# Two decoder stacks in a software pipeline: turning the queries before the scores, with the vector and GpSimd order around them rearranged

## The reference

```python
qkv = x @ Wqkv                       # 128 -> 3 * 1024, 16 heads of 64
q = l2norm(q) * qs;  k = l2norm(k) * ksc
q = q * cos * scale + rotate_half(q) * sin * scale
k = k * cos / scale + rotate_half(k) * sin / scale
sim = bq @ bk2 * 8.0                 # windows of 32 queries, 64 keys: own window and the one before
out = softmax(mask(sim)) @ bv2
x = x + out @ Wo                     # with a shift of half the features by one token
h = layernorm(x) @ W1 + b1;  a, gate = split(h)
x = x + (a * gelu(gate)) @ W2 + b2   # with the same shift
```

## Time and profile before

| | |
|---|---|
| median of 3 runs | 6443.03 us (6440.36 to 6445.80) |
| the profiled execution | 6452.24 us, of which the span of the trace is 6450.4 us |
| mean granted TensorE clock | 0.957 |
| busy in the span: PE, DVE, ACT, POOL | 88%, 71%, 53%, 66% |
| the two stacks in the trace | about 900 to 2830 us, and 4610 to 6420 us |

### The profile page before, as it was taken

One profiled execution on the slowest core, in us unless ns is written; L12 is line 12 of the kernel. 1 busy time (PEld: TensorE's weight loads), 2 busy tenths in 40 slices (PEclk: granted clock), 3 DMA queues, 4 the chain that ended last, 5 costly groups with the idle time before them and its releaser, 6 DMA issues. The chain is left out here.

```text
span 6450.4 us, 186611 instructions
## 1 busy us (share of the span) xinstructions
PE 5702.0 (88%) x76063; PEld 3949.3 (61%) x76063; DVE 4573.9 (71%) x6115; ACT 3401.8 (53%) x4021; POOL 4282.0 (66%) x2122
## 2 busy tenths in 40 slices
PE   7888968888888888889999999999688888888887
PEld 4444447666666666665555555554476666666665
DVE  6455459888888888776556555552588888888886
ACT  1444546666666666523444444434366666666664
POOL 1000058887878888526777777779688878888884
PEclk7898989999999999989999999999799999999999
DMA  0000012222222222100000000000122222222221
GB/s 25 1 1 1 2 52 63 73 61 68 67 65 67 69 60 68 49 9 1 1 1 1 1 1 1 1 1 1 52 61 75 60 74 63 72 67 68 61 68 48
DMA packets 188334, 254.69 MB, mean 39 GB/s; under 512 B 60828, under 2 KB 81816, under 8 KB 187288
## 3 DMA queue, kind: packets, MB, share of 16 engines
q1 hardware_dynamic: 187416, 242.03, 14.4%
HBM read 38.98 MB, written 1.57 MB: 6 GB/s over the span
## 5 line engine op out<-in xcount | busy, mean ns | idle before, releaser
L2094 POOL TENSOR_TENSOR XB<-XB,Pb 128x1024 f32<-128x1024 f32 x448 | 1070.4, 2389 | 338.2 <-ACT Pb L2054 297.3
L908 POOL TENSOR_TENSOR sin_qk<-raw_qk,rot 128x512 f32<-128x512 f32 x768 | 998.2, 1321 | 90.5 <-ACT raw_qk L816 59.6
L2104 DVE TENSOR_REDUCE b_pmax<-slot 128x1 f32<-128x512 f32 x1024 | 653.4, 683 | 324.9 <-PE slot L1841 323.7
L2054 ACT ACTIVATE Pb<-slot 128x1024 f32<-128x1024 f32 x512 | 502.6, 1024 | 702.1 <-PE slot L1952 649.3
L924 POOL TENSOR_TENSOR rot_out<-rot_out,sin_qk 128x1024 f32<-128x1024 f32 x192 | 604.5, 3148 | 401.3 <-DVE rot_out L982 400.3
L941 POOL TENSOR_TENSOR inv_norm<-norm2c,minus_half 128x16 f32<-128x16 f32 x192 | 668.9, 3484 | 167.8 <-DVE norm2c L1083 167.4
L530 PE MATMUL slot<-w_hi,x_hi 128*128 128x512 f32 x1152 | 547.2, 475 | 70.4 <-POOL w_lo L899 46.0
L781 ACT ACTIVATE qT<-slot 128x1024 f32<-128x1024 f32 x192 | 197.1, 1027 | 751.3 <-PE slot L537 751.3
L937 POOL TENSOR_TENSOR inv_norm<-norm2c,minus_half 128x16 f32<-128x16 f32 x192 | 559.3, 2913 | 0.0
L982 DVE TENSOR_TENSOR rot_out<-slot,rot 128x1024 f32<-128x1024 f32 x384 | 468.9, 1221 | 94.5 <-PE slot L537 52.0
L706 PE MATMUL slot<-kT,qT 64*32 64x64 f32 x24576 | 332.0, 229 | 196.2 <-issue 195.8
(11 more groups left out here) (213 smaller groups left out, 13265.8 us busy)
## 6 DMA issues: line engine op xcount, KB each, us to landing
VW<-V SPq DMA_DIRECT2D x1152, 128.0 KB
VW<-V SPq DMA_DIRECT2D x768, 64.0 KB
w_raw<-in_Wqkv SPq DMA_DIRECT2D x36, 512.0 KB, 3.7
Wo<-in_Wo SPq DMA_DIRECT2D x12, 512.0 KB, 4.2
W<-in_W SPq DMA_DIRECT2D x12, 341.0 KB, 3.1
consts<-in_shape_constants SPq DMA_DIRECT2D x1, 2436.5 KB, 9.0
QH<-rows_dram SPq DMA_DIRECT2D x128, 2.0 KB
QB<-rows_dram SPq DMA_DIRECT2D x128, 2.0 KB
```

The lines of the kernel that those rows point to most:

```text
L908: ins = pool.tensor_tensor(dst[:, :, x, :], src[:, :, 1 - x, :], tab, ALU.mult)
L2054: act.activation(Pb[:, at % B_RING, :], slot[n % 2][:, :], ACT.Exp).then_inc(s["b_exp"], 1)
L2094: pool.tensor_tensor(b_sum[:, window % 2, :], Pb[:, (at - 1) % B_RING, :] if k == 1 else b_sum[:, window % 2, :], Pb[:, at % B_RING, :], A ...
L2104: dve.tensor_reduce(b_pmax[:, n // 2, u:u + 1], o[:, 512 * x:512 * x + 512], AX.X, ALU.max)\
```

## The change

The same computation, with the same number of instructions on each engine. What it does:

- TensorE: the turn of the queries of chunk k-1 moves from behind the scores of chunk k-2 to between the value products and those scores.
- TensorE: the last of the first-layer products of a block (`value`, tile 1, into slot 2) moves ahead of the query projection.
- ScalarE: `qT` has two buffers, and its copy waits for the scores of two chunks back. The memory comes from `sq`, of which one buffer is left: the squares of queries and keys now share it.
- GpSimd: the power for the queries' norms moves ahead of the sine half of the keys.
- VectorE: the normalising of the queries moves ahead of the sum of the keys' halves and of the second residual; the third feed-forward product goes ahead of it; the four table pieces move behind `Os`; the residual XB goes ahead of the first feed-forward product.

```diff
-        sq = [sb(f"sq{i}", [128, INNER], F32, mem) for i in range(2)]
+        sq = sb("sq", [128, INNER], F32, mem)
-        qT = sb("qT", [128, 8, 128], F32, mem)
+        qT = [sb(f"qT{i}", [128, 8, 128], F32, mem) for i in range(2)]
...
# pe_stack: before the query projection of chunk 0 of the step, was behind it
+                b = at.block(9)
+                if b is not None:
+                    pe.wait_ge(s["xb_done"], START + 2 * upto(k - 4))
+                    if draining:
+                        pe.wait_ge(s["gelu_done"], START + 3 * (f + b + 1))
+                    first_layer(slot[2][0:128, 512:1024], 0, *FFN_TILES[1]).then_inc(s["value_mm"], 1)
...
# pe_stack: between value products and scores, was behind the scores
+                c = at.chunk(1)
+                if c is not None:
+                    pe.wait_ge(s["qn_done"], START + g + c + 1)
+                    wait_for_slot2()
+                    turn(slot[2], rot_out[0]).then_inc(s["tq_mm"], 1)
...
-                                           qT[r:r + 64, h // 2, 32 * w:32 * w + 32],
+                                           qT[c % 2][r:r + 64, h // 2, 32 * w:32 * w + 32],
...
# act_stack
-                    act.wait_ge(s["cq_done"], START + g + c)
-                    act.activation(sq[0][:, :], raw[0], ACT.Square).then_inc(s["q_evac"], 1)
+                    act.wait_ge(s["ck_done"], START + g + c)
+                    act.activation(sq[:, :], raw[0], ACT.Square).then_inc(s["q_evac"], 1)
...
-                    act.wait_ge(s["s_mm"], START + g + c)
-                    act.activation(qT[:, :, :].rearrange("p j t -> p (j t)"), slot[2][:, :], ACT.Copy)\
+                    act.wait_ge(s["s_mm"], START + (max(g + c - 1, 0) if isinstance(g, int) else g + c - 1))
+                    act.activation(qT[c % 2][:, :, :].rearrange("p j t -> p (j t)"), slot[2][:, :], ACT.Copy)\
...
-                    act.wait_ge(s["ck_done"], START + g + c)
-                    act.activation(sq[1][:, :], raw[1], ACT.Square).then_inc(s["k_evac"], 1)
+                    act.wait_ge(s["cq_done"], START + g + c + 1)
+                    act.activation(sq[:, :], raw[1], ACT.Square).then_inc(s["k_evac"], 1)
...
# pool_stack: ahead of sin_half(1, c, "bk_done"), was behind it
+                    pool.wait_ge(s["nq_done"], START + g + c + 1)
+                    pool.wait_ge(s["qn_done"], START + g + c)
+                    pool.tensor_tensor(inv_norm[0][:, :], norm2c[0][:, :], minus_half[:, 0:H], ALU.pow)\
+                        .then_inc(s["iq_done"], 1)
```

More of the change, by code:

```diff
@@ L652, in step @@
                     project_in(slot[0], c % 4, 0).then_inc(s["q_mm"], 1)
-                b = at.block(9)
-                if b is not None:
-                    pe.wait_ge(s["xb_done"], START + 2 * upto(k - 4))
-                    if draining:
-                        pe.wait_ge(s["gelu_done"], START + 3 * (f + b + 1))
-                    first_layer(slot[2][0:128, 512:1024], 0, *FFN_TILES[1]).then_inc(s["value_mm"], 1)
                 b = at.block(4)
@@ L710, in step @@
                     mm.then_inc(s["s_mm"], 1)
-                c = at.chunk(1)
-                if c is not None:
-                    pe.wait_ge(s["qn_done"], START + g + c + 1)
-                    wait_for_slot2()
-                    turn(slot[2], rot_out[0]).then_inc(s["tq_mm"], 1)
                 c = at.chunk(1)
@@ L934, in step @@
                     sin_half(1, c, "bk_done")
-                    pool.wait_ge(s["nq_done"], START + g + c + 1)
-                    pool.wait_ge(s["qn_done"], START + g + c)
-                    pool.tensor_tensor(inv_norm[0][:, :], norm2c[0][:, :], minus_half[:, 0:H], ALU.pow)\
-                        .then_inc(s["iq_done"], 1)
                     pool.wait_ge(s["nk_done"], START + g + c + 1)
@@ L1026, in step @@
                     dve.wait_ge(s["q_evac"], START + g + c + 1)
[L1027 removed]
+                    dve.tensor_reduce(norm2[0][:, :], heads(sq[:, :]), AX.X, ALU.add).then_inc(s["cq_done"], 1)
                     dve.wait_ge(s["cq_done"], START + g + c + 1)
@@ L1051, in step @@
                     dve.reciprocal(row_inv[:, :], row_sum[:, :]).then_inc(s["inv_done"], 1)
-                b = at.block(9)
-                if b is not None:
-                    hide(layer, f, b, 0)
                 c = at.chunk(5)
@@ L1063, in step @@
                                           slot[2][p, 512:640], ALU.add).then_inc(s["xb_done"], 1)
+                b = at.block(9)
+                if b is not None:
+                    hide(layer, f, b, 0)
                 b = at.block(7)
@@ L1083, in step @@
                     dve.tensor_scalar(norm2c[1][:, :], norm2[1][:, :], 1e-24, None, ALU.max).then_inc(s["nk_done"], 1)
-                b = at.block(5)
-                if b is not None and hi > 0:
-                    following = layer + DEPTH * call + call + b // NB + 1
-                    dve.wait_ge(s["scales_in"], START + 96 * (following + 1))
-                    dve.wait_ge(s["bq_done"], START + 4 * (f + b + 1))
-                    dve.wait_ge(s["bk_done"], START + 4 * (f + b + 1))
-                    for i, name in enumerate(names_of):
-                        col = slice((b % NB) * 4 * DH, (b % NB + 1) * 4 * DH)
-                        dve.tensor_tensor(rot[i][:, col].rearrange("p (c d) -> p c d", d=DH),
-                                          const(name)[:, col].rearrange("p (c d) -> p c d", d=DH),
-                                          qk_scales[:, i:i + 1, :].to_broadcast([128, 4, DH]), ALU.mult)\
-                           .then_inc(s["tables_done"], 1)
+                b = at.block(10)
+                if b is not None:
+                    hide(layer, f, b, 2)
+                c = at.chunk(2)
+                if c is not None:
+                    dve.wait_ge(s["rq_done"], START + g + c + 1)
+                    dve.wait_ge(s["iq_done"], START + g + c + 1)
+                    normalise(0, "qn_done")
                 c = at.chunk(2)
@@ L1114, in step @@
                                                  in1=XB[p, cols], op0=ALU.add, op1=ALU.add).then_inc(s["f_done"], 1)
-                c = at.chunk(2)
-                if c is not None:
-                    dve.wait_ge(s["rq_done"], START + g + c + 1)
-                    dve.wait_ge(s["iq_done"], START + g + c + 1)
-                    normalise(0, "qn_done")
-                b = at.block(10)
-                if b is not None:
-                    hide(layer, f, b, 2)
                 c = at.chunk(0)
@@ L1140, in step @@
                                       .to_broadcast([128, 8, 2, DH]), ALU.mult).then_inc(s["on_done"], 1)
+                b = at.block(5)
+                if b is not None and hi > 0:
+                    following = layer + DEPTH * call + call + b // NB + 1
+                    dve.wait_ge(s["scales_in"], START + 96 * (following + 1))
+                    dve.wait_ge(s["bq_done"], START + 4 * (f + b + 1))
+                    dve.wait_ge(s["bk_done"], START + 4 * (f + b + 1))
+                    for i, name in enumerate(names_of):
+                        col = slice((b % NB) * 4 * DH, (b % NB + 1) * 4 * DH)
+                        dve.tensor_tensor(rot[i][:, col].rearrange("p (c d) -> p c d", d=DH),
+                                          const(name)[:, col].rearrange("p (c d) -> p c d", d=DH),
+                                          qk_scales[:, i:i + 1, :].to_broadcast([128, 4, DH]), ALU.mult)\
+                           .then_inc(s["tables_done"], 1)
             def hide(layer, f, b, nth):
```

3 lines of the change are left out of this document (1 added, 2 removed).

## The result

The changed kernel takes 6416.45 us (median of 6 runs, 6404.30 to 6425.83) against 6441.10 us for the kernel before in the same comparison (6 runs, 6433.59 to 6445.80): ratio 0.9967, 95% interval 0.9953 to 0.9981. It is faster by 25 us by the medians, and by 21 us by the ratio (12 to 30 us by its interval). The forecast was 62 us: the sign is right, the size is two and a half times too large or more.

The account below looks back on a forecast made before the run. PE was taken as the bound, DVE 46 us behind in a stack. Per four steps, gains of 1.94 us less 0.48 and 0.16 left 1.3; 48 times that, 62 us, gave 6381 us from 6443, range 6310 to 6450.

Parts of the forecast that it names:

- The stops: PE idle inside the scores, read as instructions not yet arrived: 195.8 us at 172 places, to fall to some 60 us.
- The turn in the way: Rival, chance 0.13: stops inside scores stay unfilled, every row maximum comes 0.84 us later; median 6494 us, up to 6540.
- 0.84 - 0.84 + 0.74 + 0.84 = 1.58 us: Turn's gain over four steps: stops filled in first, third and fourth, gain given back in the second.
- needed so that the turn does not wait: VectorE normalises queries ahead of the keys' sum (1.15 us); claimed to cost nothing.
- +0.36: Fourth step of each block: value projection no longer waits 0.36 us for `Os`, with the tables now behind it.
- DVE takes over: Rival, chance 0.17: VectorE's work between row maxima is no shorter, fourth step's gain is lost; 6420 to 6445 us.
- XB: Early first-layer product waits 0.95 us for this residual; half charged, 0.48 us per four steps.
- XA: Second residual, now behind the normalising, ends after the mask needs it: 0.16 us charged per four steps.
- The power of the queries' norms: On GpSimd, moved ahead of the keys' sine half: claimed free, since POOL does both in any case.
- Normalised too late: Rival counted into the slower case (0.13): turn waits for `qn_done` before the scores; normalising expected to end near 5644.2.
- If the turn of the queries shows waits for `rot_out`: Sign at the turn of the queries on PE: such waits would show the prediction wrong; no size given.
- Busy times unchanged: Sign: the engines' busy times would stay as in the kernel before.

Follow-up runs that it names:

- e8_cos_first_apart: Changed kernel with tables before the keys' sum, queries' cosine product before the row maximum, GpSimd's queries' sum held until keys are normalised: 6310.75 us, ratio 0.9780.
- e1_tables_between: Changed kernel with the four table pieces between the queries' normalising and the keys' sum instead of behind `Os`: 6390.18 us, ratio 0.9903 to the kernel before.
- e12_between_turn_back: Changed kernel with tables between the queries' normalising and the keys' sum, and the queries' turn back behind the scores: 6439.89 us, ratio 0.9983 to the kernel before.
- e9_power_late: Changed kernel with the power for the queries' norms back behind GpSimd's sine half of the keys: 6475.32 us, ratio 1.0028 to the kernel before.
- e2_turn_back: Changed kernel with the turn of the queries back behind the scores, all else as changed: 6479.44 us, ratio 1.0038 to the kernel before.
- e3_cos_first: Changed kernel with the queries' cosine product ahead of the row maximum on VectorE: 6496.73 us, ratio 1.0067 to the kernel before.

## Why the prediction was right in sign and wrong in size

**The stops.** Right in kind: the turn between value products and scores fills the stops, and without it they come back (180.6 us). The turn in the way, the slower rival, is out: the wait inside the scores is still 1.09 us at a place (112.9 over 104), but the places fell from 172 to 104, and the stops in front of turns and mask fell too. I had looked for about 60 us left; it is 113. The page "Runtime: NRT & Kernel Launch" of the Trainium skill, section "Instruction fetch mechanics", says that the fetch is hidden; by that there would have been nothing to fill. The stops that the turn filled, 126 matmuls with their weight loads apart, speak against it here, if they are the fetch, as I read them.

**The first step that failed: how far the turn's gain reaches.** "The value projection, key projection and turn of the keys all start 0.84 us sooner." The value projection does; the key projection doesn't, since it waits for the queries' cosine product, which stands on VectorE behind the row maximum, and that chain begins at the scores' end. My terms for the turn came to 0.84 - 0.84 + 0.74 + 0.84 = 1.58 us, 76 us in all; measured 46 to 52 us. The small waits of the weight loads, 32.9 us at 140 places, are of the size of the 24 to 30 us that are missing. With the cosine product first they are gone, and the way from value to key projection is back at 2.29 us (median, e8_cos_first_apart; 2.52 in e1_tables_between, 2.30 in the kernel before); but that version gains 79 us over e1_tables_between, so more than this way is in it. A second new wait is as large: the turn of the queries waits for its normalised rows, 28 us in e1_tables_between and 4 in e12_between_turn_back, and the prediction had "needed so that the turn does not wait" at no cost. Other waits became shorter with the turn between, the mask's for the second residual by 13 us, and no run divides the missing part between the two.

**The second and larger: the tables.** "+0.36" because the value projection no longer waits for `Os` behind them: 17 us of gain. That wait did go (6.7 us to nothing in the profile). But I moved the tables at the length that they had, 1.46 us, and did not ask what GpSimd does at the new place: there one piece stands through two sine products, and four take 3.56 us, in front of the maximum. Measured: 41 us of loss, a term off by 58 us and by its sign. This is more than what separates 25 us from 62. With the tables back in front of the keys' sum the gain is 63 us, and that this is nearly the forecast is luck: the turn gave 24 us less than its term and the +17 us are not in it, and against that, where 31 us were charged for XB and XA, the rest of the change brought 11 (the sum below).

**DVE takes over**, the rival with 0.17, named the place ("the tables are still in front of the next maximum") but not the mechanism, and its 6420 to 6445 is nearly where the median fell. It and the forecast both held in part: what was right about it is that VectorE's order between scores and key projection decides.

**XB**: charged with 23 us, it is 1.8 us at 5 places, and 12.7 us at 52 on the weight load alone. XB stands on VectorE ahead of the first feed-forward product now, which I did not take into account. **XA**: charged with 8 us, the mask waits for it 18.1 us at 31 places. **The power of the queries' norms**: costed at nothing, it is worth some 39 us within this order. It brings no gain over the kernel before, whose power was late as well; it keeps one from being lost, since in this order the clip L1030 would take 1093 ns in the mean, where it took 462 in the kernel before. **Normalised too late** for the turn: I gave it a place among the slower cases at an end of 5644.2 in one step; over all steps the turn of the queries waits 29 us at 46 places, 26 more than before. "If the turn of the queries shows waits for `rot_out`" was named as a sign of being wrong, and it came.

The sum by what was measured: turn +52, tables -41, everything else (residuals, product, one `sq`, order of normalising) 0.17%, +11 in the kernel with turn and tables both back: 22 us, where the change measured 25 (0.33% of 6441 is 21).

**Signs.** The `qT` wait moved to the value copy as foreseen (751.3 to 101.7, values at 613.4, 121 before), the keys' copy stayed (86.3 to 85.9). "Busy times unchanged" failed by 43 us on VectorE, and that row was the first sign: tables 83 us more, the clip of the keys' norms (L1083) 62 more (179 to 504 ns in the mean), the splitting of x 46 less (542 to 304), the clip of the queries' norms 36 less. The maxima waited 277 us and not 242, and with the tables in front of the keys' sum it is 345: VectorE has slack there in the steps without tables.

## What to carry to other kernels

When an operation moves in an engine's order, its length must be looked up again against what the other engines do at the new place: 1.46 us became 3.56, and a 16-column instruction of 0.17 us became 1.1. When work is taken from behind a step, follow each engine from that step to the next thing that the bound engine waits for; the longest of these ways, not the work removed, says how much sooner it starts. An edit that loses can hide one that gains: the cosine product first lost 1% alone, and with one wait on GpSimd and the tables out of its way it is part of the best version here (0.978).

## What the runs showed of the hardware

Where VectorE has both inputs in SBUF and GpSimd is in a sine product or a sum, the two exclude each other for whole instructions here. Whoever starts first runs at its own length, and the other stands until it is done: normalising (both inputs in SBUF) took 1.2 us with GpSimd's sum starting 0.25 us later, which then took 3.20 us instead of 2.39; started 0.9 us after the sum, normalising took 2.59 us. Of the four table pieces the longest took 2606 ns against a median of 415:

```profile
L1137 DVE TENSOR_TENSOR rot<-consts,qk_scales x176: 405/415/2606, 997.7 to 6251.6; 128x256 f32<-128x256 f32 x176
```

Operations with one input in PSUM (`Os`, the cosine product) and row sums keep 1.20 to 1.23 us over all their instructions in the changed kernel, beside GpSimd or not. Beside GpSimd's power VectorE is not held up either: in e1_tables_between four table pieces took 1.45 us from 5254.22, within a power of 3.86 us from 5253.21. The Trainium skill, page "SBUF — State Buffer", section "Who interferes with whom", says this: a VectorE instruction with two SBUF inputs contends with a GpSimd instruction that reads SBUF, issue order decides which of them blocks, and reductions never do. The sine products and sums here agree with it; the power, by the numbers just given, did not hold VectorE up. The clip L1030, with one input of 16 columns, stands as well: 1093 ns in the mean in e9_power_late, where it takes 174 at its shortest.

The mean granted clock of TensorE rose from 0.957 to 0.964 with the turn in between, and is 0.958 with the turn back (e2_turn_back, e12_between_turn_back). The turn's place is not all that sets it: e3_cos_first has the turn in between, too, and was granted 0.957. The second product of the projections, the same 1152 instructions in each, shows what that is worth:

```profile
L531 PE MATMUL slot<-w_lo,x_hi 128*128 128x512 f32 x1152 | 466.1, 405 | 0.0
```
```profile
L531 PE MATMUL slot<-w_lo,x_hi 128*128 128x512 f32 x1152 | 459.4, 399 | 0.0
```

The first is of the kernel before, the second of the changed one: 1.4% shorter in the stacks. So a part of the 46 to 52 us that the turn's place is worth may come from the higher granted clock; that it does, and how large the part is, no run here separates.
